# Gathers of the first message stage: a coarser wait, read from a table of finished visits

## The reference, cut to what matters

```python
Ht = jnp.einsum('tmh,nh->tnm', A, h)              # 8 edge types: one message row per node and type
msg = Ht[edge_type, edge_src]                     # one row of 64 numbers per edge
m_agg = jax.ops.segment_sum(msg, edge_dst, num_segments=N)
```

## Time and profile before

| | us |
|---|---|
| three runs | 8288.54, 8300.23, 8313.96 |
| median | 8300.23 |
| the profiled execution | 8314.69 |
| its span, first to last instruction | 8312.9 |
| first gather issued / first message matmul | 230.5 / 307.4 |
| last gather issued / last message matmul | 2877.5 / 2946.9 |
| POOL L774: 1,664 gathers, busy | 1643.6 |
| PE L1208: 3,520 matmuls, busy | 860.7 |
| DVE L1662: 1,760 additions, busy | 389.7 |

### The profile page before, as it was taken

The page is one execution under the profiler, slowest core; times in us unless marked ns, Lnnn a source line. Parts: engine busy times, 40 slices in busy tenths (PEclk is TensorE's granted clock), DMA queues, the critical chain, the costliest instruction groups (busy, mean ns, idle before and its releaser), DMA issues.

```text
span 8312.9 us, 183284 instructions
## 1 busy us (share of the span) xinstructions
PE 5362.9 (65%) x33595; PEld 4316.2 (52%) x33596; DVE 4680.8 (56%) x20491; ACT 1991.8 (24%) x5537; POOL 5000.7 (60%) x10349
## 2 busy tenths in 40 slices
PE   5433555555533476676666666666668888888885
PEld 2233333333333355566555556656557777777663
DVE  3566677677633373222222222222269999999997
ACT  3000000000000042222222222222235555555553
POOL 0466666666666535666666666656657777777772
PEclk8655555555555576666666666666678898888999
DMA  6222222222222213222222222222233333333332
GB/s 217 48 50 47 46 45 46 45 46 45 46 49 51 51 58 114 87 87 86 84 83 82 83 82 82 82 81 82 82 116 94 94 94 95 93 94 95 94 94 72
DMA packets 1127950, 649.03 MB, mean 78 GB/s; under 512 B 782017, under 2 KB 1031667, under 8 KB 1126900
## 3 DMA queue, kind: packets, MB, share of 16 engines
q1 hardware_dynamic: 989540, 412.36, 20.4%
q0 software_dynamic: 137728, 233.30, 10.0%
q10 hardware_dynamic: 608, 2.55, 0.1%
HBM read 360.62 MB, written 311.42 MB: 81 GB/s over the span
## 4 chain that ended last, share of the span: by engine, by line
issue 18%; PE 15%; another core or an unknown queue 9%; DVE 7%; POOL 7%; ACT 3%; DVEq 1%; DMA 1%; POOLq 1%; SPq 0%; ACTq 0%
PE banks L1294 6%; PE banks L1296 4%; DVE h L1920 2%; PE banks L1341 2%; DVE h L1925 1%; PE banks L1295 1%; ACT ring L993 1%; DVE ring L1931 1%; ACT ring L1000 1%; PE banks L1282 1%; POOL ring L863 1%; DVE acc L1916 1%; DMA rows_by_src<-ring 1%; POOL ring L847 1%
## 5 line engine op out<-in xcount | busy, mean ns | idle before, releaser
L802 POOL DMA_INDIRECT rows_by_src<-ring x1760 | 1753.8, 996 | 1142.0 <-ACT ring L1000 618.4
L774 POOL DMA_INDIRECT wide<-msg_table,ring x1664 | 1643.6, 988 | 1196.7 <-issue 561.6
L1294 PE MATMUL banks<-wide,ring 128*128 x3520 | 1221.6, 443 | 706.5 <-ACT ring L993 393.0
L1208 PE MATMUL banks<-wide,ring 128*128 x3520 | 860.7, 426 | 570.7 <-DVE acc L1662 191.9
L1294 PEld LDWEIGHTS banks<-wide,ring 128*128 128x128 f32 x3520 | 817.7, 285 | 776.2 <-issue 775.3
L1208 PEld LDWEIGHTS banks<-wide,ring 128*128 128x128 f32 x3520 | 783.9, 328 | 656.4 <-issue 655.7
L1296 PE MATMUL banks<-h,ring 128*128 x3520 | 945.6, 361 | 143.5 <-issue 143.2
L1888 DVE COPY ring<-ring 128x4 f32<-128x4 f32 x440 | 78.8, 179 | 1669.6 <-DMA rows_by_src<-ring 1582.1
L1296 PEld LDWEIGHTS banks<-h,ring 128*128 128x128 f32 x3520 | 822.0, 285 | 243.2 <-issue 125.9
L1662 DVE TENSOR_TENSOR acc<-acc,banks 128x64 f32 x1760 | 389.7, 221 | 836.4 <-issue 315.3
L1000 ACT COPY ring<-banks 128x416 f32<-128x416 f32 x880 | 404.4, 514 | 1741.4 <-remote 1061.7
(11 more groups left out here) (322 smaller groups left out, 10373.6 us busy)
## 6 DMA issues: line engine op xcount, KB each, us to landing
h<-rows_by_src SPq DMA_DIRECT2D x1776, 105.0 KB, 2.0
ring<-attr_turned SPq DMA_DIRECT2D x440, 128.0 KB
attr_turned<-ring SPq DMA_DIRECT2D x416, 96.0 KB
rows_by_src<-ring POOLq DMA_INDIRECT x1760
wide<-msg_table,ring POOLq DMA_INDIRECT x1664
msg_table<-ring SPq DMA_DIRECT2D x100, 256.0 KB, 2.0
ring<-attr_by_dst SPq DMA_DIRECT2D x208, 64.0 KB
attr_turned<-ring SPq DMA_DIRECT2D x208, 64.0 KB
```

Source lines behind the costliest of these rows:

```text
L774: g.indirect_dma_start(out=A_g[:, b * GV + u, :], out_offset=None, in_=table[:, :], in_offset=bass.IndirectOffsetOnAxis(ap=A_idx[:, s, u:u ...
L802: g.indirect_dma_start(out=rows_d[:, :], out_offset=bass.IndirectOffsetOnAxis(ap=B_pos[:, s, u:u + 1], axis=0), in_=B_row[:, s, u, :], in_ ...
L1208: last = mm(bank[s][:, u * HID:(u + 1) * HID], A_D[:, s, u, :], A_g[:, ds(r[u], 1), :].rearrange("p a k -> p (a k)"), start=True, stop=True)
L1294: mm(b[:, 0:H1], B_DT[:, t, u, :], q_tab[:, w, :].rearrange("p a k -> p (a k)"), start=True, stop=False)
```

## The change: what it does

POOL no longer waits for `a_mm` before every group of four tiles. The first 32 groups (the first filling of the ring) have no such wait at all. From the 33rd group on, before every fourth group, POOL loads a number from a new table `wread` and waits for `a_mm` to reach it: the number of visit groups after which the sixteen tiles that the next sixteen gathers overwrite are all read. The table is made in the setup: DVE computes, for each window and each group of tiles, how many of the window's visits lie before the group's end (`done_w`, two instructions on 100 x 416), PE adds over the windows with one matmul, and DVE rounds up to groups (two instructions on one row of 416). POOL waits for `s_done` once before the 33rd group. The first loop turn of POOL is written out apart from the loop over the other twelve. The other two waits per group stay as they were.

```diff
+        groups_mem = sb("groups", [64, VGROUPS], i32)
+        wfirst, wread = groups_mem[0:1, :], groups_mem[32:33, 0:TILE_GROUPS]
+        tile_end, done_w = (acc_flat[:, k:k + TILE_GROUPS] for k in (5500, 5500 + TILE_GROUPS))
...
             def gather(i):
                 for b in range(KEPT // GV):
                     s = b % NS
+                    if s == 0 and not first(i):
+                        read = pool.value_load(wread[0:1, ds((i - 1) * (KEPT // GV) + b + NS - 1, 1)], min_val=1, max_val=VGROUPS)
+                        pool.wait_ge(a_mm, read)
+                        turn(pool, "pool")
                     if not (first(i) and b < NS):
                         pool.wait_ge(a_g[s], 16 * GV * (i * (KEPT // BODY) + b // NS))
-                    if not (first(i) and b < 7):
-                        pool.wait_ge(a_mm, i * (KEPT // GV) + b - 6)
                     pool.wait_ge(a_idx, i * (KEPT // GV) + b + 1)
...
-            loop(pool, TILES // KEPT, gather)
+            gather(0)
+            pool.wait_ge(s_done, 4)
+            with pool.Fori(1, TILES // KEPT) as i:
+                gather(i)
...
+            pe.wait_ge(s_done, 2)
+            mm(bank[4][0:1, 0:TILE_GROUPS], ones[0:N_KEYS, 0:1], done_w[0:N_KEYS, :], start=True, stop=True).then_inc(s_done, 1)
...
+            dve.wait_ge(s_iotav, 1)
+            v.tensor_scalar(tile_end[:, :], iota_v[:, 0:TILE_GROUPS], float(GV), float(GV), ALU.mult, ALU.add).then_inc(s_done, 1)
             visit_table(0)
...
+            dve.wait_ge(s_done, 1)
+            ch.link(v.tensor_scalar(done_w[0:K, :], tile_end[0:K, :], small[0:K, 22:23], nt[0:K, :], ALU.subtract, ALU.min))
+            v.tensor_scalar(done_w[0:K, :], done_w[0:K, :], 0.0, None, ALU.max).then_inc(s_done, 1)
             dve.wait_ge(s_kl, BLOCKS)
             for q in range(4):
...
+            dve.wait_ge(s_done, 3)
+            ch.link(v.tensor_scalar(wread, bank[4][0:1, 0:TILE_GROUPS], float(GV - 1), None, ALU.add))
+            v.tensor_scalar(wread, wread, 2, None, ALU.arith_shift_right).then_inc(s_done, 1)
             dve.wait_ge(r_c, REC0)
```

More of the change, by code:

```diff
@@ L189, in build @@
         wwin, wtile, wslot, woff = (visits[32 * k:32 * k + 1, :] for k in range(4))
-        wfirst = sb("wfirst", [1, VGROUPS], i32)
+        groups_mem = sb("groups", [64, VGROUPS], i32)
+        wfirst, wread = groups_mem[0:1, :], groups_mem[32:33, 0:TILE_GROUPS]
         wgot = sb("wgot", [1, VTAB // BODY], i32)
@@ L397, in build @@
         s_bd, s_bp = sem("s_bd"), sem("s_bp")
-        n_in, s_fold, s_dev = sem("g1_in"), sem("s_fold"), sem("s_dev")
+        n_in, s_fold, s_dev, s_done = sem("g1_in"), sem("s_fold"), sem("s_dev"), sem("s_done")
         a_D, a_mm = sem("a_D"), sem("a_mm")
```

## The result

The changed kernel takes 8828.1 us (8823.8 to 8838.7, four runs) where the kernel before took 8307.1 beside it: ratio 1.063 [1.061, 1.066], 521 us slower. The prediction was 8427 with a range up to 8600. The profiled execution took 8824.3, 509.6 more than that of before.

| stretch | before, us | after, us | difference | forecast |
|---|---|---|---|---|
| first message matmul at | 307.4 | 434.4 | +127 | +45, and +2 for the added work |
| 25 counting turns | 616.9 | 673.3 | +56 | +60 |
| 52 ranking turns | 1345.1 | 1671.3 | +326 | +50 |
| 26 turns after ranking, and the rest of the stage | 677.5 | 688.5 | +11 | -30 |
| all that follows the stage | 5366.0 | 5355.1 | -11 | 0 |

The account below looks back on a forecast made before the run. The first message stage was taken to go at DVE's and PE's pace, starved by long unbroken runs of POOL's gathers. +45 + 60 + 50 - 30 + 2 = +127 on 8314.7, less 14.5, gave 8427 us, range 8215 to 8600.

Parts of the forecast that it names:

- signs: POOL's first long idle near 391 us, 16-gather runs, under 0.6 additions per us, SP moves at 0.7 us, last gather after 2877.
- Counting turns, +60: First message stage: 16-gather runs slow the additions while counting; +60 us, between -109 and +94.
- Ranking turns, +50: Ranking turns: only runs beginning behind SP's stores escape slowing, like an earlier 18-gather run; +50 us, between -139 and +200.
- Start, +45: Setup and first loops: the first 128 gathers run unbroken to about 391 us and slow DVE; +45 us, 0 to 70.
- Added work, +2: Table setup, register loads and POOL's one wait: only DVE's last two instructions stand on the path; 2 us with latencies.
- After ranking, -30: Turns after ranking: runs already have sixteen gathers and POOL has fewer left; -30 us, between -102 and +60.
- The rule on shared descriptor generation: DVE and SP would slow together while SP issues DMAs; by it alone the start term, some 45 us, would go.
- slower, and worse: Rival: all high ends but the last, +70 + 94 + 200, giving 8660 us, or 8560 with two; chance 0.13.
- Faster: Rival: the ring was the bound, in gather waits or POOL's pauses after ranking; 50 to 90 us gained, about 8220; chance 0.22.
- no change: Rival: POOL merely runs ahead and later waits as long, with stalls at their share; 8300 us, chance 0.15.

Follow-up runs that it names:

- e11: Kernel before, plus POOL waiting after every second group of four gathers until that group's rows have landed; ratio 0.9970 where the kernel before took 8232 us.
- e3: Changed kernel, with POOL held once at the eighth group until the first message matmul; ratio 1.061 where the kernel before took 8313 us.
- e1: Changed kernel with the old wait per group put back beside the new one; ratio 0.9975 where the kernel before took 8313 us.
- e4: Changed kernel with the exact wait before every group and POOL held once for the first message matmul; ratio 1.0065 where the kernel before took 8313 us.
- e5: Kernel before with its constant wait made only before every second group; ratio 1.0011 where the kernel before took 7260 us.
- e15: Kernel before plus five small POOL operations after every second group, a 2.3 us pause; ratio 1.0006 where the kernel before took 8228 us.
- e10: Changed kernel, exact wait only before every eighth group, POOL held once for the first message matmul; ratio 1.103 where the kernel before took 8232 us.
- e6: Changed kernel, exact wait only before every eighth group, POOL held once for the first message matmul; ratio 0.9989 where the kernel before took 7260 us.

## Why the prediction was wrong

The direction was right, and so was the cause (long runs of gathers hold up the others); what failed is the size of two terms, the ranking turns above all. Most signs that it named came: POOL's first long idle time at 392 us, runs of sixteen gathers, rates below 0.6, the last gather at 3391.6 us, the rest of the kernel unchanged. SP's moves did not tell the two kernels apart. The wait for landed rows wasn't the bound (e11 adds such waits and loses nothing). Term by term:

- *Counting turns, +60.* Right: +56. The two runs of the earlier trace rows (10.5 additions on average) were a fair sample: the changed kernel's 16-gather runs in these turns have 11.7.
- *Ranking turns, +50.* This is the term that failed: +326, beyond its own high end of +200. The step was "only the one that begins behind SP's stores to go like rows 8", and the rate of a slowed stretch taken from the counting turns. In the changed kernel the 45 runs of sixteen gathers in these turns hold 6 additions in 20.3 us on average, not 15, and their last 9 us go at 0.01 to 0.19 per us, not 0.28. The run of the earlier trace rows was no stroke of luck: the kernel before has five such runs in its ranking turns, and all hold 13 to 15 additions. But they are another kind of run. Their sixteen gathers (not 18, as the prediction has it) take some 22.3 us, because short breaks remain in them; in the earlier trace rows two gathers start late:

```profile
1786.32 1.36 POOL L774 DMA_INDIRECT wide<-msg_table,ring  x1 [1.17 <-issue]
...
1797.56 0.94 POOL L774 DMA_INDIRECT wide<-msg_table,ring  x1 [0.82 <-issue]
```

Between its other gathers POOL idles 0.30 us, as everywhere inside the changed kernel's runs. The other four runs have the same two or three breaks of 0.8 to 1.2 us, never more than eight gathers apart. So no unbroken run of sixteen was there to be read in the old ranking turns, and the high end was the counting turns' slowdown (15%) carried over. Whether these short breaks spare the five runs, or the place in the turn where they begin, is not isolated; nor is why ranking turns suffer more than counting turns (more rounds between engines for the same sixteen visits is a likely reason).
- *Start, +45.* Too low: the measured +127 lies beyond its end of +70. The forecast added 1.2 us to each DVE instruction, from an early stage of the slowing. Deeper in the run the price is some 22 us for each round between DVE and PE: five such rounds and two shorter ones stood on the path, with 137 us of idle time before them. e3 shows that a hold merely moves this price.
- *Added work, +2.* Right: L1652, L1653, L1659 and L1660 take 0.49, 0.38, 0.58 and 0.37 us, and e1 measures nothing.
- *After ranking, -30.* Here +11, with the rest of the stage. With fine waits (e4) this stretch does gain some 40 us, so the gain exists and the coarse wait ate it. (The 23.9 us per turn that the prediction gives for it is 23.5 in the trace; the sum doesn't use it.)
- *The rule on shared descriptor generation.* The Trainium skill (Perfetto Trace Analysis, "DMA Instruction — HWDGE (DVE, Sync)") says that the DVE and Sync sequencers share the block which generates hardware DMA descriptors. Read as in the prediction, it would have the slowing come with SP's DMAs. Between 271 and 396 us SP issues none, and DVE's rounds take 22 us all the same; and where the kernel before takes 7260 us SP issues as many in e5 with no slowing. As the cause of this loss the rule falls.

Of the rivals, "slower, and worse" had the right kind of size and 0.13, but its ends for the start and the ranking turns were still too low. Its "8560 with two of them" doesn't come out of the sum either: two of the three high ends give 8464 to 8594. "Faster" and "no change" are refuted for this kind of chip, while on the other one gathers are the bound, though by POOL's pace and not by the ring's wait.

What stays open is what in a long run of gathers slows the others, and why one kind of chip doesn't show it. No chip was used twice as far as the record names them, so that the two kinds are a lasting property of the chips isn't shown either. The runs show that it ends when no gather is issued (e11, e15) and grows with the run (e10). On the slower kind the best versions are e11 and e1, both 0.3% or less ahead; e11 costs 6% on the other, e1 was not run there.

## What to carry to other kernels

Thinning out a wait also lengthens the run of whatever it used to interrupt: if other engines slow down beside that run, its small waits are breathing space, and their idle time must not be booked as a gain. Where a rate falls with the age of a run, read it for every kind of stage and from all runs, not from one or two, and give the high end from the worst age seen. Compare the spacing inside a sample run with the spacing that the change will make: a run with short breaks in it says little of one without. And see on more than one chip what the kernel before takes, before a few per cent are taken for a property of the code.

## What the runs showed of the hardware

- The same kernel took 7252 to 8313 us by the chip it ran on, a larger span than any change here. The difference lies in the two stages where POOL issues indirect DMAs: in e6 the last message matmul came at 2446 us against 2947 before, and L802's 1,760 transfers (L811 in e6) took 2327 us from first to last against 2881; together 1055 of 1058 us.
- On the slower kind, deep in an unbroken run of gathers, a round between two engines takes 22 us instead of 1.5, and SP's register moves, 29 ns at the median, take up to 1427 ns. On the other kind a run of 1,636 gathers shows nothing of it (e6), and no move of the stage takes more than 29 ns (e5).
- Recovery is quick in the stage (2 to 5 us after the last gather, additions come at 1.05 per us in the changed kernel's ranking turns) and slow after 161 us of gathers: the round then under way still took 13.4 us of idle time, ending 18 us after POOL had stopped.
